# Expert tiles of two 64-row halves, one expert each, in a mixture-of-experts block

## The reference

```
logits = flat @ router_w.T                       # 1024 x 16
_, topk_idx = top_k(logits + router_bias, 2)     # two experts of 16 for each token
...
for e in range(16):
    h = silu(flat @ Wu[e]) * (flat @ Wg[e])      # 256 -> 128
    out = out + combine[:, e:e + 1] * (h @ Wd[e])   # 128 -> 256
out = out + silu(flat @ Su) * (flat @ Sg) @ Sd   # a shared expert, 256 -> 256 -> 256
x = x + tanh(g_ffn) * out
```

## Time and profile before

| | us |
|---|---|
| median of 3 runs | 210.04 |
| lowest and highest | 208.91 and 210.41 |
| the profiled execution, by its own time | 208.32 |
| its span in the profile | 206.2 |

### The profile page before, as it was taken

How to read it: one execution, slowest core, us unless ns; L and a number is a source line. 1 busy time by engine, 2 the same in 40 slices (tenths; PEclk the granted TensorE clock), 3 DMA queues, 4 the chain that set the end, 5 groups by cost and what they waited for, 6 DMA issues and landing times.

```text
span 206.2 us, 3739 instructions
## 1 busy us (share of the span) xinstructions
PE 177.2 (86%) x988; PEld 130.1 (63%) x988; DVE 143.7 (70%) x464; ACT 104.7 (51%) x280; POOL 86.9 (42%) x123
## 2 busy tenths in 40 slices
PE   0287999999999997986757989889999999999962
PEld 0165546666766663854436877658888888886841
DVE  6987999989888898889797773643443333441494
ACT  2063568594786554652416320127777777775100
POOL 7067546211323244151726757102665555666100
PEclk9999999999999998799965585999999999999997
DMA  4899999999999910000200122171555445531494
GB/s 114 252 412 426 423 419 412 423 416 394 264 350 369 399 47 0 3 0 2 76 28 26 54 77 104 51 179 53 158 160 170 158 161 164 164 104 79 140 368 153
DMA packets 19318, 39.96 MB, mean 194 GB/s; under 512 B 2625, under 2 KB 14338, under 8 KB 17122
## 3 DMA queue, kind: packets, MB, share of 16 engines
q1 hardware_dynamic: 16112, 32.18, 44.2%
q0 software_dynamic: 2256, 6.18, 7.9%
q10 hardware_dynamic: 930, 1.38, 2.1%
HBM read 15.46 MB, written 24.27 MB: 193 GB/s over the span
## 4 chain that ended last, share of the span: by engine, by line
PE 36%; DVE 24%; issue 17%; POOL 15%; ACT 3%; DMA 1%; ACTq 1%; POOLq 0%; DVEq 0%
POOL y_tok L477 13%; DVE prob L849 10%; PE ps_pv L1192 8%; PE ps_edge L1282 6%; PE ps_edge L1176 4%; PE ps_nat L1203 3%; PE ps_feat L1156 3%; PE ps_nat L1118 3%; PE ps_rows L1139 2%; DVE stats L809 2%; PE ps_feat L1223 1%; PE ps_edge L1321 1%; DVE x_res L1034 1%; DMA y_tok<-pv_t,y_row 1%; PE ps_nat L1165 1%
## 5 line engine op out<-in xcount | busy, mean ns | idle before, releaser
L849 DVE SCALAR_TENSOR_TENSOR prob<-ps_edge,t_nat,mask_t 128x256 f32<-128x256 f32 x128 | 53.7, 474 | 3.2 <-PE ps_edge L1176 1.8
L477 POOL DMA_INDIRECT y_tok<-pv_t,y_row x31 | 29.7, 959 | 31.8 <-issue 19.4
L1192 PE MATMUL ps_pv<-prob,feat 128*33 128x256 f32 x256 | 36.1, 406 | 2.1 <-DVE prob L849 2.0
L1321 PE MATMUL ps_edge<-up_w,xt 128*128 x124 | 32.0, 381 | 0.3 <-ACT xt L671 0.3
L1018 DVE SCALAR_TENSOR_TENSOR mask<-mask,ps_edge 128x128 f32<-128x128 f32 x31 | 8.9, 287 | 29.1 <-ACT mask L677 28.2
L1321 PEld LDWEIGHTS ps_edge<-up_w,xt 128*128 128x128 f32 x124 | 21.2, 190 | 2.2 <-issue 0.6
L1176 PE MATMUL ps_edge<-rows_r,sel_row 128*128 128x256 f32 x64 | 17.0, 354 | 5.3 <-DVE prob L849 5.0
L1192 PEld LDWEIGHTS ps_pv<-prob,feat 128*33 128x33 f32 x256 | 12.6, 114 | 13.6 <-issue 3.4
L1282 PE MATMUL ps_edge<-x_t,up_w 128*128 128x256 f32 x64 | 19.8, 471 | 0.0
L406 POOL TENSOR_TENSOR rows_r<-rows_q,rows_h 128x256 fp32r<-128x256 f32 x8 | 5.8, 729 | 32.7 <-ACT rows_h L539 32.7
L1176 PEld LDWEIGHTS ps_edge<-rows_r,sel_row 128*128 128x128 f32 x64 | 10.6, 209 | 13.6 <-DVE prob L849 7.4
(11 more groups left out here) (178 smaller groups left out, 344.0 us busy)
## 6 DMA issues: line engine op xcount, KB each, us to landing
x_rows<-x_t SPq DMA_DIRECT2D x16, 1024.0 KB, 16.6
mask_t<-x_rows SPq DMA_DIRECT2D x31, 129.0 KB
up_w<-in_wu SPq DMA_DIRECT2D x1, 2048.0 KB, 30.6
up_w<-in_wg SPq DMA_DIRECT2D x1, 2048.0 KB, 12.0
down_w<-in_wd SPq DMA_DIRECT2D x1, 2048.0 KB, 10.7
x_res<-in_x SPq DMA_DIRECT2D x3, 256.0 KB, 4.4
out<-x_res SPq DMA_DIRECT2D x3, 256.0 KB, 2.1
prob<-y_tok SPq DMA_DIRECT2D x2, 256.0 KB, 3.8
```

What stands on the lines that cost most here:

```text
L477: pool.indirect_dma_start(y_tok[:], bass.IndirectOffsetOnAxis(y_row[:, j % R_SLOTS:j % R_SLOTS + 1], 0), y_sb[:, j % Y_SLOTS, :], None).th ...
L849: last = dve.scalar_tensor_tensor(prob[:, n % 4, c, :], ps_edge[n // 2 % 2][:, h % 2, :], t_nat[:, k % 2, c, 0, h:h + 1], mask_t[:, a, c, ...
L1192: last = pe.matmul(ps_pv[at:at + HO, j, :], feat[:, k % 2, c, h, :], prob[:, (HEADS * k + h) % 4, c, :], start=(c == 0), stop=(c == C - 1))
L1321: last = pe.matmul(to, xt[:, j % 2, c, :], up_w[:, bass.ds(e, 1), :, c * P:(c + 1) * P], start=(c == 0), stop=(c == C - 1))
```

## The change

A tile is made of two halves of 64 rows, and each half has an expert of its own. Experts fill half tiles, at most 1024 x 2 / 64 + 16 = 48 of them, so 24 tiles. The first half takes its weights from `up_w` and `down_w` by a register, as before; the second half's weights are copied by VectorE, two tiles ahead, to one of five slots (`up_now`, `down_now`). Each up and down matmul becomes two with 64 columns of weights. The table is worked out and turned earlier. Each tile is loaded with two DMAs of 64 rows.

```diff
+HALF = P // 2
+X_SLOTS, Y_SLOTS, R_SLOTS, W_SLOTS, W_AHEAD = 7, 4, 8, 5, 2
-    TILES = TOKENS * TOP // P + EXPERTS - 1
+    TILES = (TOKENS * TOP // HALF + EXPERTS) // 2
@@ sync: load_tile
-                if j % 8 == 0:
-                    x_of[0] = nc.values_load_multi_w_load_instructions(
-                        table_i[0:1, 1, j:min(j + 8, TILES)], ...)[1]
+                if j % 4 == 0:
+                    x_of[0] = [nc.values_load_multi_w_load_instructions(
+                        table_i[0:1, 1, i * TILES + j:i * TILES + j + 4], ...)[1]
+                        for i in range(2)]
...
-                sp.dma_start(x_in[:, j % X_SLOTS, :], x_rows[bass.ds(x_of[0][j % 8], P), :]
-                             ).then_inc(tile_landed[j % X_SLOTS], 16)
+                for i in range(2):
+                    sp.dma_start(x_in[HALF * i:HALF * (i + 1), j % X_SLOTS, :],
+                                 x_rows[bass.ds(x_of[0][i][j % 4], HALF), :]
+                                 ).then_inc(tile_landed[j % X_SLOTS], 16)
@@ vector: tables
-                F = N // P * B
+                F = TOKENS // HALF
@@ vector
+            def pick_weights(j, e):
+                if j >= W_SLOTS:
+                    dve.wait_ge(y_done, j - W_SLOTS + 1)
+                mark(dve.tensor_copy(up_now[:, j % W_SLOTS].rearrange("p k f -> p (k f)"),
+                                     up_w[:, bass.ds(e, 1), :, :].rearrange("p s k f -> p (s k f)")))
+                settle()
+                dve.tensor_copy(down_now[:, j % W_SLOTS], down_w[:, bass.ds(e, 1), :].rearrange("p s d -> p (s d)")
+                                ).then_inc(picked, 1)
@@ vector: order
             positions(3)
+            tables()
             shared_step(1)
-            tables()
+            whole_tables()
             shared_step(2)
-            whole_tables()
             base(0)
             shared_step(3)
+            dve.wait_ge(up_landed, 64)
+            dve.wait_ge(down_landed, 32)
+            dve.wait_ge(table_i_ready, 1)
...
+            load_experts(0)
+            for j in range(W_AHEAD):
+                pick_weights(j, of_tile[j])
             base(1)
             for j in range(TILES):
+                if j % 8 == 4 and j + 4 < TILES:
+                    load_experts(j // 8 + 1)
+                if j + W_AHEAD < TILES:
+                    pick_weights(j + W_AHEAD, of_tile[j + W_AHEAD])
                 tile_hid(j)
                 result_rows(j)
@@ tensor
             def tile_up(j):
+                pe.wait_ge(picked, j + 1)
                 pe.wait_ge(xt_out, j + 1)
...
                 for c in range(C):
-                    last = pe.matmul(to, xt[:, j % 2, c, :], up_w[:, bass.ds(e, 1), :, c * P:(c + 1) * P],
-                                     start=(c == 0), stop=(c == C - 1))
+                    for i in range(2):
+                        rows_at = slice(HALF * i, HALF * (i + 1))
+                        last = pe.matmul(ps_edge[j % 2][rows_at, 0, :].rearrange("p (k f) -> p k f", k=2),
+                                         xt[:, j % 2, c, rows_at],
+                                         up_w[:, bass.ds(experts[j], 1), :, c * P:(c + 1) * P] if i == 0 else
+                                         up_now[:, j % W_SLOTS, :, c * P:(c + 1) * P],
+                                         start=(c == 0), stop=(c == C - 1))
...
-                pe.matmul(ps_y[j % 2], ht_r[:, j % 2], down_w[:, bass.ds(e, 1), :], start=True, stop=True
-                          ).then_inc(y_done, 1)
+                for i in range(2):
+                    rows_at = slice(HALF * i, HALF * (i + 1))
+                    last = pe.matmul(ps_y[j % 2][rows_at], ht_r[:, j % 2, rows_at],
+                                     down_w[:, bass.ds(experts[j], 1), :] if i == 0 else down_now[:, j % W_SLOTS, :], start=True, stop=True)
+                last.then_inc(y_done, 1)
@@ tensor: order
             up(1)
+            turn_table()
             up(2)
             down(1)
-            turn_table()
             up(3)
...
             down(2)
+            turn_tile(0)
             down(3)
-            turn_tile(0)
```

More of the change, by code:

```diff
@@ L78, in flamingo_block @@
         seen_f = sb("seen_f", [P, EXPERTS])
-        fills = sb("fills", [P, EXPERTS, N // P * B])
+        fills = sb("fills", [P, EXPERTS, TOKENS // HALF])
         upto = sb("upto", [P, EXPERTS, EXPERTS])
@@ L189, in flamingo_block @@
         xt = sb("xt", [P, 2, C, P])
+        up_now = sb("up_now", [P, W_SLOTS, 2, C * P])
+        down_now = sb("down_now", [P, W_SLOTS, D])
         th_r, hid_r = (mask[:, i, :].rearrange("p (b q) -> p b q", b=2) for i in range(2))
@@ L261, in flamingo_block @@
         xt_done, xt_out, ug_done = sem("xt_done"), sem("xt_out"), sem("ug_done")
+        picked = sem("picked")
         th_done, hq_done, h_done = sem("th_done"), sem("hq_done"), sem("h_done")
@@ L449, in router_constants @@
                 for tile, pattern, base, along in (
-                        (seen_f, [[TOKENS // P, EXPERTS]], 0, 0), (fills, [[TOKENS, EXPERTS], [P, N // P * B]], 0, 0),
-                        (tile_no, [[0, 1]], 0, 1), (tile_row, [[0, 1]], 0, P), (spare, [[P, Y_SLOTS]], 0, 1)):
+                        (seen_f, [[TOKENS // P, EXPERTS]], 0, 0), (fills, [[TOKENS, EXPERTS], [HALF, TOKENS // HALF]], 0, 0),
+                        (tile_no, [[0, 1]], 0, 1), (tile_row, [[0, 1]], 0, HALF), (spare, [[P, Y_SLOTS]], 0, 1)):
                     pool.iota(tile[:], pattern=pattern, base=base, channel_multiplier=along,
@@ L1079, in _, with load_experts @@
             positions(3)
+            tables()
             shared_step(1)
-            tables()
+            whole_tables()
             shared_step(2)
-            whole_tables()
             base(0)
             shared_step(3)
+            dve.wait_ge(up_landed, 64)
+            dve.wait_ge(down_landed, 32)
+            dve.wait_ge(table_i_ready, 1)
+            of_tile = []
+            def load_experts(n):
+                of_tile.extend(nc.values_load_multi_w_load_instructions(
+                    table_i[0:1, 0, TILES + 8 * n:TILES + 8 * n + 8], engines=[mybir.EngineType.DVE], min_val=0,
+                    max_val=EXPERTS - 1,
+                    skip_runtime_bounds_check_because="tables() takes the smaller of it and the last expert")[1])
+            load_experts(0)
+            for j in range(W_AHEAD):
+                pick_weights(j, of_tile[j])
             base(1)
             for j in range(TILES):
+                if j % 8 == 4 and j + 4 < TILES:
+                    load_experts(j // 8 + 1)
+                if j + W_AHEAD < TILES:
+                    pick_weights(j + W_AHEAD, of_tile[j + W_AHEAD])
                 tile_hid(j)
@@ L1307, in turn_tile @@
             def turn_tile(j):
-                pe.wait_ge(tile_landed[j % X_SLOTS], 16 * (j // X_SLOTS + 1))
+                pe.wait_ge(tile_landed[j % X_SLOTS], 32 * (j // X_SLOTS + 1))
                 if j >= 2:
@@ L1313, in turn_tile, with tile_up @@
                 last.then_inc(xt_done, 1)
-            def tile_up(j, e):
+            def tile_up(j):
+                pe.wait_ge(picked, j + 1)
                 pe.wait_ge(xt_out, j + 1)
@@ L1329, in turn_h, with tile_down @@
                 pe.transpose(ps_ht[j % 2], h_r[:, j % 2], ident[:]).then_inc(ht_done, 1)
-            def tile_down(j, e):
+            def tile_down(j):
                 pe.wait_ge(hto_done, j + 1)
@@ L1394, in _ @@
                 if j < TILES:
-                    tile_up(j, experts[j])
+                    tile_up(j)
                 if j % 8 == 4 and j + 4 < TILES:
@@ L1400, in _ @@
                 if 0 <= j - 2 < TILES:
-                    tile_down(j - 2, experts[j - 2])
+                    tile_down(j - 2)
             for s in range(EARLY, SHARED_STEPS):
```

12 lines of the change are left out of this document (5 added, 7 removed).

## The result

| | before | after |
|---|---|---|
| median, us | 209.75 | 212.09 |
| lowest and highest | 208.91 to 210.41 | 211.52 to 214.25 |
| runs | 4 | 4 |
| span of the profiled execution | 206.2 | 210.1 |

The changed kernel takes 1.020 of the time (95% interval 1.012 to 1.027): it is slower, by 2.3 us at the medians. A second set of 12 runs, made with the experiments, has a median of 211.55 beside 209.15 for before, with a ratio of 1.009 (1.005 to 1.013). So the loss is between 1 and 2%, and its size is no better known than that. A single kernel's executions lie up to 8 us apart (before: 206.6 to 214.7 in 46 runs). The ratios are taken from undisturbed runs alone, and they differ from the quotients of the medians by up to 0.9% (here 1.020 and 1.011).

What follows compares the result with a forecast made beforehand. TensorE was taken to bound the loop at 1.63 us a tile. Loop +1.1 and front +2.0 gave +3.1 us, from 210.04 to a median of 213.1; own range 212 to 215.5, 8 in 10 within 206.5 to 216.5.

Steps and rivals of the forecast that it cites:

- the second rival: Switching costs as priced but the front costs little (clock up at 129.0 or copies of 0.5): 211.5 to 212; chance 0.25.
- Loop: Tile loop on TensorE: seven tiles less save 11.4 us, switching adds 0.57 a tile, +12.5 over 22 intervals: +1.1 us.
- Copies: VectorE's two weight copies a tile: 0.9 us, VectorE 1.6 us a tile in all, hidden by TensorE's 2.20.
- GpSimd's stores longer by 0.5 to 1 us a tile: Indirect stores in the loop may grow beside VectorE's copies, to 1.8 to 2.2 us a tile, still within 2.20.
- Doubled loads: SP's two loads per tile, 0.52 us of issue each, 1.04 in a period of 2.20: hidden.
- Front: Ahead of the loop: start 1.9 to 2.0 us later, 1.3 from the late clock and the rest from copies.
- a sign of being wrong: A clock that falls again in the pauses before tile 1 would make the forecast wrong: then 3 us more.
- Ending: Behind the loop nothing changes: the stores' last interval, the DMA of 2.37 and the ending stay.
- switching is hidden: Rival: whole to split without loss on TensorE, a tile 1.63 to 1.7 us: 201 to 203 us; chance 0.18.
- The copies as the pace: Rival: VectorE or GpSimd sets the loop's pace, by slow copies or copies waiting for stores: 218 or 221; chance 0.10.
- the halves in series: Rival: split halves run one after the other on TensorE, 1.3 us a tile, 28 in all: 241; chance 0.02.

Runs made afterwards that it cites:

- one trip: Changed kernel with TensorE's order turn_tile(j+1), turn_h(j-2), up(j), down(j-2), so two changes between whole and split a tile, not four: 205.83 us, ratio 0.989.
- both amendments: Changed kernel with the order turn_tile(j+1), turn_h(j-2), up(j), down(j-2), and turn_tile(0) behind down(3) again: 204.88 us, ratio 0.977.

## Why the prediction was right, and where it wasn't

The forecast was 213.1 us, 3.1 slower, and the result is 212.1, slower by 2.3 at the medians. The span was to be 209.3 and is 210.1. In the second set the median is 211.55 and the ratio, 1.009, gives 1.9 us. So the direction is right and the size is at the lower edge: 212.09 is at the foot of the forecast's own 212 to 215.5, and 211.55 lies where the second rival had it.

**Loop: right, and its mechanism shown.** Period 2.224 for a predicted 2.20; a change costs 0.15 us in each direction, twice in and twice out for each tile. The sum of +1.1 became +0.81, with errors that partly cancel: the price was 0.597 for 0.57, of the 22 intervals only 20 are full, and of the partial ones two grew by 0.2 to 0.3 and one shrank. The Trainium skill (TensorEngine Tiling (Array Packing), Theoretical Speedup) offers up to 2x for weights of at most 64 columns. The pairs 0.01 us apart agree with it; the period shows no gain, since a tile's 15 records take as long as the 9 of before plus four changes. What the same page of the Trainium skill says under Key Properties, that a change of the tiling mode drains TensorE, has no price there. The traces agree with a gap of 0.09 to 0.10 us at each change, and 0.15 in all decided the case.

**Copies: hidden, as said, and cheaper.** 0.43 + 0.29 us; with the wait between them 0.86 from the start of the first to the end of the second, so 0.9 was near. From 512 to 256 elements the duration falls by 0.136 us, 0.53 ns an element.

**GpSimd's stores longer by 0.5 to 1 us a tile: wrong.** 23 of the 24 kept 0.96, and one took 1.01. In the steady loop the copies are over 0.26 us before a store starts. Where they do meet, in the kernels with whole products and with one trip, the effect is small and goes either way: at most 0.20 us on a store, 0.16 on a copy, and often nothing. The step that failed took the effect of L867 and L871 for that of any copy in SBUF. The Trainium skill (SBUF — State Buffer, Who interferes with whom) has copies among the instructions that can lock the shared port, with the other engine blocked for the whole instruction. The runs agree with it in part: they show contention, but not such a block, since a copy ran its usual 0.43 us inside a store of 0.96. That it is the two SBUF inputs of L867 and L871 that matter is argued, not shown.

**Doubled loads: hidden in the loop, not in front.** Two loads a tile cost TensorE nothing at a period of 2.22. But with `turn_tile(0)` back behind `down(3)` tile 1 was waited for, 0.84 to 0.93 us in three kernels. The prediction weighed 1.04 us of issue against the period alone and had no term for the first tiles.

**Front: +1.93 for 2.0 in the result's profile, and that match is luck.** In the repeated profile it went as written: a late clock at 132.2 (132.3 predicted), up(3) through at 134.75 (134.9), and copies and `base(1)` in a row, to 140.50: +1.28 instead of +1.9, mostly since three tiles' copies on the path took 0.77 each for 0.9 (0.4 in all), the register load 0.63 for 0.7 and `base(1)` 0.60 for 0.69. In the profile that belongs to the result the chain was another: the clock rose early, and the gain of it went to a wait that I had left out. `turn_tile(0)` stands ahead of `down(3)`, and its tile can't be loaded before the last scatter is done. SyncE had the table by 128.6 and passed its wait for that scatter at 132.6; before, its first loads went out at 133.2, so of the 3.6 us by which the table was earlier, the load gained 0.4. `down(3)` was queued behind the 2.07 us, and then the clock fell. The prediction had named such a fall as a sign of being wrong, at 3 us more. It lasted 3.4 us here, in which TensorE ran at half its speed, so it cost 1.7 at most. The changes around the first up products, 0.3 us, had no term either. That the pause made it fall isn't shown, as it stayed up after 1.61 to 1.79 us in three other profiles. The rule that I broke is to ask of each moved step what its input still waits for. What this wait costs on average is open: taking it away gave 211.55 to 210.89, which overlaps, and the pattern of clock rises changes from one execution to the next. The first two table steps have 256 elements, not 512 (0.42 each, not 0.69), so the transpose came at 127.6 for 127.9. And up(1) ended at 126.7 and 127.2 for 126.4. The pause between them was 0.91 and 0.40 us for 1.5.

**Ending: predicted at nothing, +1.1 in the profile.** 0.2 of it is the last tile's two changes. The other 0.9 is the clock, which fell 0.5 us before the last additions; before, they were over before it fell. It doesn't go with the splitting: the additions took about 2.05 us in the profile of the kernel with one trip, but 1.10 as before in those without copies (four changes a tile), with whole products, and with both amendments. Why it falls where it does I have not tested.

**Rivals.** That switching is hidden (0.18) fell with the periods 1.63, 1.92, 2.22. Its other price was near, though: it said that at half the loss the time would be 207, and the kernel with half the changes has 205.8. The second rival, switching as priced with a cheap front (0.25, 211.5 to 212), can't be told from the forecast by time: the two medians are 212.09 and 211.55. Its condition of an early clock held in the result's profile, at 126.4, but the front wasn't cheap there. The copies as the pace (0.10) and the halves in series (0.02) fell.

## What to carry to other kernels

Splitting TensorE's array by columns lets two products run side by side, but each change between whole and split costs about 0.15 us here, as much as 0.7 of a 256-column step of f32; count the changes in the written order, and group the work by mode before anything else. Fewer, fuller tiles paid 11.4 us and four changes a tile took back 12. With two changes the kernel was 1.1% faster than before, and 2.3% with `turn_tile(0)` moved back as well. A step that is moved ahead gains only what its latest input allows, and whatever stands behind it in the queue then waits too. And when two chains in front of a loop end within a microsecond of each other, one profile shows only the one that was last that time: here it was tile 0's load, then the copies behind a late clock, then tile 1's load.

## What the runs showed of the hardware

- A change between 128 and 64 columns of weights costs 0.15 us (f32, 256 columns moving, clock at its upper level): periods of 1.63, 1.92 and 2.22 us with 0, 2 and 4 changes. Of it 0.09 to 0.10 is a gap; the rest is in the first matmul behind it, which is 0.05 to 0.06 longer (L1362's first record 0.43 for 0.38, L1351's two 0.44 for 0.38). That this part is its weights' loading is argued, not shown.
- Two f32 streams on the column halves run pairwise without loss, a pair in 0.21 to 0.22 us, also when one's moving operand has a register in its address and the other's has not.
- An indirect store of GpSimd and an f32 copy of VectorE within SBUF disturb each other little. A copy of 0.43 us inside a store of 0.96 left both at their length; at most the store took 1.16, or a copy of 128x256 0.45 for 0.29. The same kind of store took 1.44 for 0.96 beside two VectorE instructions with two SBUF inputs.
- The granted clock rose at 126.4 in one execution and at 132.2 in another of the same kernel on the same work, and this moved TensorE by about 2 us at `down(2)` (132.57 and 134.74).
